# The order of TensorE's four kinds of work in a step of the second attention

## The reference

```python
x = L0_attn_x                                   # (4, 1024, 128)
x = x + ga * _L0_attn_ref(...)                  # causal, 16 heads of 64
x = x + gb * _L0_ffn_ref(...)                   # attention and MLP on 127 chosen tokens
h = _layernorm(x) * (1 + ca) + sa
# _L1_attn_ref: 16 heads of hd = 8, N = 1024, no mask
q, k, v = heads(h @ Wq + bq), heads(h @ Wk + bk), heads(h @ Wv + bv)
q, k = _apply_3d_rope(q, ...), _apply_3d_rope(k, ...)
attn = softmax(einsum('bhqd,bhkd->bhqk', q, k) * hd ** -0.5)
x = x + ga * (einsum('bhqk,bhkd->bhqd', attn, v) ... @ Wo + bo)
x = x + gb * _L1_ffn_ref(...)                   # 8 experts, top 2
```

## Time and profile before

| | |
|---|---|
| median of 3 runs | 2799.43 us (2799.24 to 2804.2) |
| the profiled execution | 2801.26 us, span 2799.5 us, mean granted clock 0.905 |
| busy | PE 79%, PEld 32%, DVE 58%, ACT 46%, POOL 29% |
| chain that ended last | PE 62%, DVE 21%, ACT 9%, issue 5%, SP's queue 2% |
| costliest lines of the chain | PE L875 60% (every matmul goes through this helper), DVE L2342 6%, ACT L1765 4% |
| the second attention's four stretches | 1063 us in all |

### The profile page before, as it was taken

How to read it: one execution, slowest core, us unless ns; L and a number is a source line. 1 busy time by engine, 2 the same in 40 slices (tenths; PEclk the granted TensorE clock), 3 DMA queues, 4 the chain that set the end, 5 groups by cost and what they waited for, 6 DMA issues and landing times.

```text
span 2799.5 us, 39653 instructions
## 1 busy us (share of the span) xinstructions
PE 2208.8 (79%) x14753; PEld 898.0 (32%) x14757; DVE 1628.7 (58%) x2829; ACT 1274.6 (46%) x2289; POOL 804.5 (29%) x618
## 2 busy tenths in 40 slices
PE   3989998898777778888767678798868677567776
PEld 2434443444221133444322123344422122121112
DVE  3454456556667456555676735646575865576622
ACT  1433333333357643333357763243326465347762
POOL 1655554343300033443511114344423000001103
PEclk9999999999999898989989998898979898779978
DMA  3000010001110000000210001001110100200000
GB/s 77 15 22 23 15 42 22 12 27 44 39 39 1 1 29 12 22 27 12 64 39 20 12 4 37 12 12 37 38 39 23 46 1 16 84 7 5 5 1 8
DMA packets 81199, 69.14 MB, mean 25 GB/s; under 512 B 46672, under 2 KB 62800, under 8 KB 80496
## 3 DMA queue, kind: packets, MB, share of 16 engines
q1 hardware_dynamic: 81008, 66.60, 8.6%
HBM read 57.58 MB, written 8.98 MB: 24 GB/s over the span
## 4 chain that ended last, share of the span: by engine, by line
PE 62%; DVE 21%; ACT 9%; issue 5%; SPq 2%; DMA 1%; POOL 0%; ACTq 0%; POOLq 0%; DVEq 0%
PE banks L875 60%; DVE pmax L2342 6%; ACT ring L1765 4%; DVE part_max L1943 2%; ACT room L1572 1%; SPq L666 1%; DVE ntmp L1892 1%; PE banks L1014 1%; DVE pick L2083 1%; DVE rstd L1894 1%; DVE room L2092 1%; DVE ntmp L1847 1%; DVE h L1911 1%; DVE stats L1899 1%; DVE oT L1964 1%
## 5 line engine op out<-in xcount | busy, mean ns | idle before, releaser
L816 POOL TENSOR_TENSOR p_sum<-p_sum,ring 128x1024 f32<-128x1024 f32 (+3 forms) x320 | 549.3, 1716 | 806.3 <-PE banks L875 452.4
L2342 DVE TENSOR_REDUCE pmax<-banks 128x2 f32<-128x1024 f32 x512 | 611.1, 1222 | 227.6 <-PE banks L875 225.1
L875 PE MATMUL banks<-ring,v 128*9 128x512 f32 (+4 forms) x2816 | 578.0, 601 | 0.0
L1943 DVE TENSOR_REDUCE part_max<-banks 128x2 f32<-128x1024 f32 (+3 forms) x384 | 365.6, 958 | 335.0 <-PE banks L875 332.4
L875 PE MATMUL banks<-qT,kT 64*128 64x512 f32 (+4 forms) x2048 | 469.8, 522 | 103.1 <-DVE pmax L2342 53.1
L1765 ACT ACTIVATE ring<-banks 128x512 f32<-128x512 f32 x768 | 416.3, 597 | 188.7 <-PE banks L875 187.4
L1524 ACT ACTIVATE ring<-banks 128x1024 f32<-128x1024 f32 (+3 forms) x320 | 245.8, 768 | 472.9 <-PE banks L875 467.8
L875 PE MATMUL banks<-oT 64*128 64x512 bf16 x1024 | 192.3, 414 | 122.5 <-ACT ring L1765 91.8
L875 PEld LDWEIGHTS banks<-qT,kT 64*128 64x128 f32 (+1 forms) x2048 | 146.8, 168 | 379.6 <-issue 120.7
L847 POOL TENSOR_TENSOR room<-room 128x512 f32<-128x512 f32 x32 | 40.6, 1268 | 733.3 <-ACT room L1572 733.3
L875 PE MATMUL banks<-p_sum,v 128*9 128x512 f32 (+1 forms) x768 | 218.4, 646 | 30.2 <-DVE oT L1964 25.2
(11 more groups left out here) (270 smaller groups left out, 2665.9 us busy)
## 6 DMA issues: line engine op xcount, KB each, us to landing
inv_bc<-softmax_inverses SPq DMA_DIRECT2D x64, 256.0 KB, 3.9
w_qk<-in_L_attn_w_qkv SPq DMA_DIRECT2D x64, 64.0 KB, 2.1
low<-in_L_ffn_attention_mask SPq DMA_DIRECT2D x4, 1024.0 KB, 5.8
stage<-rope_constants SPq DMA_DIRECT2D x4, 1024.0 KB, 4.8
x_b<-in_L_attn_x SPq DMA_DIRECT2D x4, 512.0 KB, 4.6
w_v<-in_L_attn_w_qkv SPq DMA_DIRECT2D x32, 64.0 KB, 2.1
stage<-in_L_ffn_w SPq DMA_DIRECT2D x8, 256.0 KB, 6.1
out<-x_b SPq DMA_DIRECT2D x16, 128.0 KB, 1.8
```

Of the source, the lines that this page charges most:

```text
L816: pool.tensor_tensor(sv, sv, ring0[SLOT[m]][:, :, 0:HALF - lo], ALU.add).then_inc(sem("added"), 1)
L875: return pe.matmul(dst, lhsT, rhs, start=start, stop=stop)
L1943: dve.reduce_max(part_max[:, :, t, c], banks[MAX_PAIR[m]][:, :, 0:w], AX).then_inc(sem("row_max"), 1)
L2342: dve.reduce_max(pmax1[:, :, g, t, c], banks[(0, 3)[USE1[b]["max", m] % 2]][:, :, :], AX).then_inc(sem("row_max1"), 1)
```

## The change

TensorE's order in a step changes. Before: product for the maximum, two score products for the exponentials, row maxima (where the step has them), value products (even steps). After: product for the maximum, row maxima, value products, and last the two score products. What follows (transposes, output projection, side steps) stays behind all four. No instruction is added or removed, each keeps its own wait, and no other engine's order changes.

```diff
             def step1(b, k, steps=None):
                 if k + LEAD < STEPS1:
                     max1_item(b, k + LEAD)
+                if k + LEAD in ROWS_AT:
+                    max1_to_rows(b, ROWS_AT[k + LEAD])
+                if k > 0 and k % 2 == 0:
+                    pv1_items(b, k // 2 - 1)
                 if k + 1 >= 0:
                     for n in range(2 * k + 2, 2 * k + 4):
                         if n < NI1:
                             st1_item(b, n)
-                if k + LEAD in ROWS_AT:
-                    max1_to_rows(b, ROWS_AT[k + LEAD])
-                if k > 0 and k % 2 == 0:
-                    pv1_items(b, k // 2 - 1)
                 if k in CTX_AT:
```

## The result

The changed kernel takes 2730.05 us (median of 4 runs, 2727.07 to 2733.0) against 2799.34 us (4 runs): ratio 0.9754, 95% interval 0.9731 to 0.9777. That is 69 us less. The forecast was 44 less and its range ended 8 us short of the result: right in direction and in what the order does, too small in size.

The account below looks back on a forecast made before the run. No engine is full, so latencies between engines set the pace. Unit ends and row maxima gain 60.2 us, side steps lose 4.5, absorption takes 7.5 and 4.5: net 44, forecast 2755 us, range 2738 to 2790.

Parts of the forecast that it names:

- Parts 1 to 3: Undisturbed steps 0 us; last value products of a unit 1.07 us gained, row maxima 1.08, each at 7 places a batch.
- Plain cycle: Two undisturbed steps: stay at 2.59 us, the halves 1.52 and 1.07 changing places, 0 us gained.
- max to pv: TensorE's switch from the product for the maximum to the value products (pv), unseen before: taken as 0.32 us.
- odd st after a unit's end: Odd steps' score products (st) after a unit's last value products: next ones 2.80, 5.45, 8.34 us later; 1.07 us gained.
- rows to next odd st: Row maxima to the next odd step's score products: 4.68 us instead of 5.13, value products running inside ACT's copies.
- The wait for DVE behind the transposes: After a unit's end, the even max waits until DVE has read the transposes: at 5.97 us, not 5.67.
- the clock, left out of the sum: Value products at half clock after the row-maxima wait: up to 0.9 us at some of 28 places, for the lower end.
- the term of the side steps: Part 4: even side steps gain 0.9 us, odd ones lose 0.9; 5 odd ones too many, 4.5 us lost.
- side chains and other waits: Gains not arriving: 7.5 us in the third stretch's side chains, 4.5 us in the other stretches' waits.
- The rivals: Gains given back: 2780 us, chance 0.22; nothing moves: 2799 us, chance 0.07; slower: chance 0.09.
- the slower rival: DVE late for even maxima delays value and score products behind them: 2807 us, or 2847 with little gained; chance 0.09.
- The tiling rule: Changing tiling mode drains TensorE, 0.10 us each: 3 us less at the transposes, nearly all taken by the wait for ACT.

Follow-up runs that it names:

- the two kernels with max behind: Changed kernel with the even steps' product for the maximum behind the score products: on all even steps 2757.22 us; on plain even steps alone 2737.2 us.

## Why the prediction was wrong

- **Parts 1 to 3 held to the hundredth.** Plain cycle 2.59 for 2.59; max to pv 0.31 for 0.32; odd st after a unit's end 2.80, 5.44, 8.34 for 2.80, 5.45, 8.34; rows to next odd st 4.67 for 4.68. The wait for DVE behind the transposes is there (850.26 to 850.79, 0.53). As a whole the undisturbed unit gained 26.13 - 24.06 = 2.07 us at full clock where the sum had 2.15.
- **The step that failed: the clock, left out of the sum.** The forecast had read in the earlier trace rows that after the wait at the row maxima pv runs at half clock, noted that pv would now lie inside that wait, left this out of the sum ("I leave it out of the sum"), and put it at the lower end of the range only as up to 0.9 us at some of 28 places, at most 25 us. It priced one kind of place. In batch 3's last unit before the change, TensorE sat at half clock through the plain cycles, 3.66 us for 2.37, and the forecast had no row of that window. The kernel before gains 35 us by nothing but busy work in its waits; the change itself brought half clock in the stretches from 244 to 157 us. Taken in full, the 25 us would have brought the sum to the measured time, and by luck: 24 of the 87 us of half clock that went lie in batch 3's last unit, where there are no row maxima.
- **The second step, a smaller one: the term of the side steps was mis-sized.** "These prices change places" had 0.9 us for each. Timeline of PE after, batch 1, an expert on an odd step:

```profile
1476.70 0.39 PE L875 MATMUL banks<-kT,qT 64*128 64x512 bf16 x2 [0.47 <-ACT p_sum L1765]
1477.02 1.12 PE L875 MATMUL banks<-stage,hT 128*128 128x512 f32 x2
1478.08 0.39 PE L875 MATMUL banks<-oT 64*128 64x512 bf16 x2
...
1479.37 0.39 PE L875 MATMUL banks<-kT,qT 64*128 64x512 bf16 x2
```

  It costs 2.67 - 1.52 = 1.15 (it was 0.72 in the earlier trace rows); on an even step it still costs some 1.4. The odd price rose by 0.43 and the even one fell from 1.63 by some 0.2 only, so by these single steps 53 odd and 48 even side steps would lose 53 x 0.43 - 48 x 0.2, some 13 us where 4.5 stood (an estimate).
- **The order's sum came out near, in part by luck.** At like clock it gained 39 us in the stretches where the sum had 43.7. Batch by batch the sum had 13.6, 10.0, 8.5 and 11.8 us, and the stretches gave 12.4, 9.1, 9.8 and 7.9. If the side steps lost some 13 us, side chains and other waits took some 8 (60.2 - 13 - 39.2) where the sum allowed 12, so these two errors partly cancel; no run separates them. In the stretches the clock's 33.5 us and the order's 39.2, less the 4 us by which the rest of the profiled execution was longer, make 68 us; against the forecast's 43.7 this is the 25 us between 2755 and 2730.
- **The rivals.** The third batch gave 10 us of its 15, so some was absorbed, as taken. PE's waits on `pmax` fell from the 98 of the earlier trace rows to the 79 of this row of the changed kernel's waits (their total hardly, from 101.9 to 99.4 us), so the slower rival had no ground:

```profile
PE banks L875 <- DVE pmax L2342: 99.4, 79, 7.4
```

  Its mechanism (DVE late for a max) is real: it is what the two kernels with max behind ran into.
- **The tiling rule.** The drain that the Trainium skill (TensorEngine Tiling (Array Packing), Key Properties) states fits the trace again, 0.31 against 0.22 between a pair and pv, and the added change of shape at the transposes (849.13 to 849.45) lies in ACT's round trip, as weighed.
- **The rule on idle TensorE.** The Trainium skill (TensorE: Matmul & The Clock Gate, Why this matters for your kernels) warns of throughput lost to long idle gaps between bursts of matmuls. The trace bears out the direction (granted 0.59 in the last unit before, 1.00 once its waits were filled) but not that a long gap is needed: in that unit's plain cycle the waits were 0.68 us each. The measurement decides, and a reader who goes by long gaps alone would have priced this unit at nothing, as the forecast did.

## What to carry to other kernels

Rotating the same pieces of work in a cycle over several engines gained nothing in the plain steps here (2.59 us either way); look at the irregular ones, where another engine's copy makes a long wait that the moved work can fill. Before forecasting an edit that moves TensorE's idle time, read the granted clock stretch by stretch and price it: here it was nearly half of the result. Filling TensorE's waits with matmuls that nobody reads measures that price in one run. It paid where TensorE was on the chain and at half clock; in the lead-in it gave nothing, and six matmuls in nearly every odd step of units at full clock cost 0.25 us a unit. To compare two kernels at like clock, take stretches or units of their profiles whose granted clock is the same, not the whole times.

## What the runs showed of the hardware

- Eight matmuls of 128 columns in each odd step (0.62 us of records, where the waits were 0.68) took a stretch of 29 us from a granted clock of 0.59 to 1.00.
- Half clock on the chain costs about a third of its time here: 3.66 us against 2.37 for two steps of the same order, and 109.5 us against 104.5 for four units with and without some 14 us of it; ACT's busy time is the same in both (17.2 and 79.3 us). In the lead-in, where TensorE waits for DVE and for a load, 37 us less of it did not shorten anything.
- The time at half clock differs between kernels whose TensorE work is the same in a stretch: the first stretch, which has no side steps and is identical in the changed kernel, with even side steps, with odd ones, and with the filled lead-in, had 21, 21, 21 and 8 us of it in their profiles, at 215.9, 216.0, 215.9 and 211.5 us.
